# Starting the next stage's normalisation and weights in the tail of the stage ahead, in a four-stage f32 kernel

## The reference

```python
x = x + attention0(layernorm(x))   # linear attention with decay, 32 heads of 128, gated
x = x + ffn0(layernorm(x))         # SwiGLU, 1376 hidden, with LoRA of rank 16
x = x + attention1(layernorm(x))   # ALiBi softmax, causal, 32 heads of 16, q and k normalised
x = x + ffn1(layernorm(x))         # GELU, 2048 hidden

def _layernorm(x, axis=-1, eps=1e-05):
    m = jnp.mean(x, axis=axis, keepdims=True)
    v = jnp.var(x, axis=axis, keepdims=True)
    return (x - m) / jnp.sqrt(v + eps)
```

## Time and profile before

| | us |
|---|---|
| median of 3 runs | 2022.02 |
| lowest, highest | 2015.08, 2023.35 |
| profiled execution | 2025.39 |
| its span | 2023.7 |
| PE busy | 1916.9 |
| DVE busy | 856.4 |
| POOL busy | 610.3 |
| ACT busy | 437.1 |

### The profile page before, as it was taken

The page is one execution under the profiler, slowest core; times in us unless marked ns, Lnnn a source line. Parts: engine busy times, 40 slices in busy tenths (PEclk is TensorE's granted clock), DMA queues, the critical chain, the costliest instruction groups (busy, mean ns, idle before and its releaser), DMA issues. The chain is left out here.

```text
span 2023.7 us, 26337 instructions
## 1 busy us (share of the span) xinstructions
PE 1916.9 (95%) x10439; PEld 1504.0 (74%) x10439; DVE 856.4 (42%) x1586; ACT 437.1 (22%) x534; POOL 610.3 (30%) x692
## 2 busy tenths in 40 slices
PE   6999999999999999999999869998888999987999
PEld 5888888888888888888888758886653444456887
DVE  5242342432433333424324453313666888725611
ACT  3111111111111111111111121101313666643200
POOL 4322231321312313222300045534720212225532
PEclk9999999999999999999999979998985999998999
DMA  4010100110110100101100112201033233001111
GB/s 157 29 58 29 58 29 29 57 57 10 47 57 29 54 32 30 56 29 57 36 0 16 47 53 83 81 7 69 21 66 51 48 54 55 14 22 47 50 50 68
DMA packets 36521, 93.15 MB, mean 46 GB/s; under 512 B 7200, under 2 KB 11936, under 8 KB 31968
## 3 DMA queue, kind: packets, MB, share of 16 engines
q1 hardware_dynamic: 35172, 89.56, 15.1%
q10 hardware_dynamic: 1276, 2.62, 0.8%
HBM read 75.89 MB, written 2.10 MB: 39 GB/s over the span
## 5 line engine op out<-in xcount | busy, mean ns | idle before, releaser
L146 PE MATMUL a_ps<-a_xh_h,a_w_h 128*128 128x512 f32 x768 | 307.4, 400 | 4.3 <-POOL a_w_l L270 2.9
L148 PE MATMUL a_ps<-a_xh_h,a_w_l 128*128 128x512 f32 x768 | 301.3, 392 | 0.0
L147 PE MATMUL a_ps<-a_xh_l,a_w_h 128*128 128x512 f32 x768 | 300.7, 391 | 0.0
L60 POOL TENSOR_TENSOR tick<-neg_half 128x1 f32<-128x1 f32 x48 | 24.6, 513 | 615.7 <-PE a_ps L148 615.7
L390 DVE TENSOR_TENSOR x<-x,a_ps 128x1024 f32<-128x1024 f32 x64 | 78.2, 1221 | 259.9 <-PE a_ps L148 259.9
L1153 ACT ACTIVATE a_pr<-a_ps 128x1024 f32<-128x1024 f32 (+1 forms) x192 | 153.1, 812 | 88.3 <-PE a_ps L1366 71.4
L146 PEld LDWEIGHTS a_ps<-a_xh_h,a_w_h 128*128 128x128 f32 x768 | 145.0, 189 | 32.5 <-issue 3.3
L148 PEld LDWEIGHTS a_ps<-a_xh_h,a_w_l 128*128 128x128 f32 x768 | 144.6, 188 | 30.4
L147 PEld LDWEIGHTS a_ps<-a_xh_l,a_w_h 128*128 128x128 f32 x768 | 144.9, 189 | 27.9
L146 PE MATMUL a_ps<-a_w_h,a_xh_h 128*128 128x512 f32 x352 | 145.0, 412 | 8.7 <-POOL a_w_l L251 5.9
L1386 PE MATMUL a_ps<-a_K,a_Q 64*128 64x512 f32 (+2 forms) x384 | 136.8, 448 | 14.1 <-DVE a_mx L1261 11.5
(11 more groups left out here) (180 smaller groups left out, 3651.9 us busy)
## 6 DMA issues: line engine op xcount, KB each, us to landing
a_raw<-in_a_wqkgv SPq DMA_DIRECT2D x30, 1024.0 KB, 4.9
f_raw<-in_f_w SPq DMA_DIRECT2D x33, 320.0 KB, 2.9
a_raw<-in_a_wout SPq DMA_DIRECT2D x32, 256.0 KB
f_raw<-in_f_w SPq DMA_DIRECT2D x32, 256.0 KB, 2.6
a_cst<-in_a_cst SPq DMA_DIRECT2D x32, 129.0 KB, 2.0
...
```

The source lines that it names most:

```text
L60: nc.gpsimd.tensor_tensor(top["tick"][:, :], top["neg_half"][:, 0:1], top["neg_half"][:, 1:2], ALU.mult)
L146: nc.tensor.matmul(out, w_hi, x_hi, start=start, stop=False)
L147: nc.tensor.matmul(out, w_hi, x_lo, start=False, stop=False)
L148: return nc.tensor.matmul(out, w_lo, x_hi, start=False, stop=stop)
```

## The change

**Normalisation.** The helpers take a list of tiles. The first tiles of the next stage's normalisation (`F0_EARLY` and `F1_EARLY` four, `A1_EARLY` five) are done in the block ahead, each as soon as its part of `x` is final: DVE alternates `x_out` or `add_out`, statistics and subtractions, each `x_out` or `add_out` with a wait for its own end; the other engines get the matching steps. The rest (`..._LATE`) is done at the start of the next stage, behind PE's first products. `xh_h`, `xh_l` and the first weights (high, low and raw) become shared buffers in `top`; placeholders named `under_...` keep the stages' own buffers off them.

**First weights.** SP loads ffn0's LoRA matrix and first two weight blocks in attention0, attention1's q weights in ffn0, and the first two blocks of ffn1 in `attention1_out`; POOL splits them there, ahead of `rms` in attention0 and between the last `split_w2` in ffn0.

**Semaphores.** These steps have a second `Sems` object in attention0, ffn0 and `attention1_out`, each with its own clearing and meeting of all engines at the end.

**Output of ffn0.** The last two f are one loop over the output tiles, with the transpositions of tile i-4 behind tile i.

**Attention1.** `FIRST` is gone: m = 0 and 1 start at once, and tiles 5, 6 and 7 are transposed ahead of m = 2, 3 and 4. The q-side stacks of pairs 3 to 5 (30 transfers) are issued by SP, not by ACT. POOL clears their tiles, not DVE.

```diff
@@ attention0: SP, POOL, DVE
+            sp.wait_ge(s("proj_done"), 16 * NG)
+            sp.dma_start(top["f0_la"][:, :], a["f0_lora_a"]).then_inc(s2("la_in"), 16)
+            for w in (1, 3):
+                sp.dma_start(top[f"f0_raw{w}"][:, :], a[f"f0_w{w}"][0]).then_inc(s2(f"raw{w}_in"), 16)
             sp.wait_ge(s("attn_done"), H0)
...
+            f0_split_a(nc, pool, s2, top)
+            for w in (1, 3):
+                pool.wait_ge(s2(f"raw{w}_in"), 16)
+                f0_split_w(nc, pool, s2, top, w, 0)
             pool.wait_ge(s("ms_ready"), 1)
...
+            for t in F0_EARLY:
+                ln_gpsimd(nc, pool, s2, b, F0_EARLY, t)
...
-            for t in range(NT):
+            def x_out(t):
                 nc.vector.scalar_tensor_tensor(out=x[:, t, :], in0=acc[:, t, :], scalar=rms[:, t:t + 1],
                                                in1=x_again[:, t, :], op0=ALU.mult, op1=ALU.add).then_inc(s("x_out"), 1)
-            dve.wait_ge(s("x_out"), NT)
+                dve.wait_ge(s("x_out"), t + 1)
+            ln_vector(nc, dve, s2, b, F0_EARLY, x_out, lambda t: x_out(t + 4))
@@ ffn0: POOL, DVE, PE
             for f in range(2, NF0):
                 split_w2(f)
+                if 4 <= f < 4 + KT:
+                    split_next(f - 4)
+            for t in A1_EARLY:
+                ln_gpsimd(nc, pool, s2, b2nd, A1_EARLY, t)
...
+            ln_vector(nc, dve, s2, b2nd, A1_EARLY, add_out, lambda t: add_out(t + 3) if t >= 2 else None)
...
-            ln_tensor(nc, pe, s, b, range(4))
             lowered(0)
-            ln_tensor(nc, pe, s, b, range(4, 6))
             hidden(1, 0, 0)
-            ln_tensor(nc, pe, s, b, range(6, NT))
+            ln_tensor(nc, pe, s, b, F0_LATE, F0_LATE)
             lowered(1)
...
-            for f in range(NF0):
+            for f in range(NF0 - 2):
...
+            pe.wait_ge(s("w2_split"), NF0)
+            pe.wait_ge(s("g_split"), 2 * NF0)
+            for i in range(NT):
+                out(NF0 - 2, i)
+                out(NF0 - 1, i).then_inc(s("out_done"), 1)
+                if i >= 4:
+                    ln_tensor(nc, pe, s2, b2nd, A1_EARLY, (i - 4,))
+            ln_tensor(nc, pe, s2, b2nd, A1_EARLY, (4,))
@@ attention1_heads: SP, POOL, ACT, DVE, PE
             stack(sp, 3, 0)
+            stack(sp, 3, 1)
             max_row(1)
-            stack(sp, 4, 0)
-            stack(sp, 5, 0)
+            for p in (4, 5):
+                stack(sp, p, 0)
+                stack(sp, p, 1)
...
+            pool.wait_ge(qs("proj_done"), 3 * NT)
+            for i in range(3, SETS):
+                nc.gpsimd.memset(QT[i].bitcast(F32)[:, :], 0.0).then_inc(s("late_clear"), 1)
...
-            for p in range(3, SETS):
-                stack(act, p, 1)
...
-            pieces(1, 2, 8)
-            dve.wait_ge(qs("proj_done"), 3 * NT)
-            for i in range(3, SETS):
-                clear(i)
-            pieces(1, 8, NP)
+            pieces(1, 2, NP)
...
+            for m in range(AFTER):
+                if 2 <= m < 2 + len(A1_LATE):
+                    ln_tensor(nc, pe, qs, b, A1_LATE, (A1_LATE[m - 2],))
@@ attention1_out: DVE, PE
+            ln_vector(nc, dve, s2, b, F1_EARLY, add_out, lambda t: add_out(t + 4))
...
                 part(t, 3).then_inc(s("out_done"), 1)
+                if t >= 4:
+                    ln_tensor(nc, pe, s2, b, F1_EARLY, (t - 4,))
@@ ffn1: PE
-            ln_tensor(nc, pe, s, b, range(4))
-            pe.wait_ge(s("ln_lo"), 4)
             hidden(0, 0)
-            ln_tensor(nc, pe, s, b, range(4, NT))
-            pe.wait_ge(s("ln_lo"), NT)
+            ln_tensor(nc, pe, s, b, F1_LATE, F1_LATE)
+            pe.wait_ge(s("ln_lo"), len(F1_LATE))
             hidden(0, 1)
```

More of the change, by code:

```diff
@@ L49 @@
 NF1 = F1 // P
+ALL = range(NT)
+F0_EARLY, F0_LATE = range(4), range(4, NT)
+A1_EARLY, A1_LATE = range(5), range(5, NT)
+F1_EARLY, F1_LATE = range(4), range(4, NT)
+XH = 2 * KT * T
+EARLY = 3 * KT * D
 def split_hi(engine, hi, src):
@@ L106, in ln_gpsimd @@
-def ln_gpsimd(nc, pool, s, b, t):
-    one = slice(t, t + 1)
-    pool.wait_ge(s("ln_meanvar"), t + 1)
+    for i in range(min(ahead, len(tiles))):
+        stats(i)
+    for i, t in enumerate(tiles):
+        if i + ahead < len(tiles):
+            stats(i + ahead)
+        dve.wait_ge(s("ln_hi"), i + 1)
+        nc.vector.tensor_tensor(b["xh_l"][:, :, t * P:(t + 1) * P], b["bank"](t).rearrange("p (k q) -> p k q", k=KT),
+                                b["xh_h"][:, :, t * P:(t + 1) * P], ALU.subtract).then_inc(s("ln_lo"), 1)
+        if after is not None:
+            after(t)
@@ L138, in ln_tensor @@
+def ln_tensor(nc, pe, s, b, tiles, some):
+    for t in some:
+        pe.wait_ge(s("ln_normed"), tiles.index(t) + 1)
         for k in range(KT):
-            last = nc.tensor.transpose(b["ps"][:, t, k * P:(k + 1) * P], b["xn"][:, t % 2, k * P:(k + 1) * P],
+            last = nc.tensor.transpose(b["bank"](t)[:, k * P:(k + 1) * P], b["xn"][:, t % 2, k * P:(k + 1) * P],
                                        b["ident"][:, :])
@@ L686, in _ @@
             split_a2(0)
-            split(3, 0)
             for f in range(1, NF0):
@@ L1105, in select @@
                                         ).then_inc(s("selected"), 1)
-            for t in range(NT):
-                ln_gpsimd(nc, pool, qs, b, t)
-                if FIRST - 1 <= t < FIRST - 1 + KT:
-                    split(0, (t - FIRST + 1,))
+            for t in A1_LATE:
+                ln_gpsimd(nc, pool, qs, b, A1_LATE, t)
             split(1)
@@ L1537, in _ @@
                 sp.dma_start(raw[:, w], w_dram[:, w]).then_inc(s(f"raw_in{k}"), 16)
+            for i in range(2):
+                sp.dma_start(top["f1_raw"][:, i, :], w1_dram[i]).then_inc(s2(f"raw_in{i}"), 16)
         @block.gpsimd
```

365 lines of the change are left out of this document (200 added, 165 removed).

## The result

The changed kernel takes 2008.8 us (median of 9 runs, 1998.1 to 2011.2) where the kernel before takes 2022.3: ratio 0.992, 95% interval 0.9901 to 0.9939. Forecast were 2004.0 us and a range of 1995 to 2013. Its profiled execution took 2008.8 us, span 2007.0, so 16.6 less than the span before (2023.67 and 2007.03), where 18.0 were forecast.

What follows compares the result with a forecast made beforehand. PE, busy 95% of the span, bounds the kernel; only its idle time and half-clock work can move. Terms -0.8 - 5.6 + 0.8 - 6.4 - 6.5 + 0.5 = -18.0 us gave median 2004.0, range 1995 to 2013.

Steps and rivals of the forecast that it cites:

- Stage ends: Freeing semaphores at stage ends: 65 ranges for 29 at 0.16 us, three more meetings at 0.3, +6.7 us of PE idle.
- Attention0 to ffn0: From attention0's end to `lowered(1)`: DVE's chain takes 1.6 and 1.4 us a tile, `lowered(1)` starts earlier, -0.8 us.
- `lowered(1)` starts at 1197.95: In ffn0, after 5.2 us for tiles 4 to 7, `lowered(1)` starts at 1197.95 for 1198.75.
- Ffn0 to attention1: From ffn0's end to attention1's first clip: -7.3 us, with 1.7 of clock loss -5.6; bounds -8 and -2.5.
- I charge another 1.7: In ffn0, a clock loss of 1.7 us behind PE's new 2.2 us stall before step 9.
- Heads: In attention1, with the stacks on SP, PE's 6.36 us idle before the third score go: -6.4 us, bounds 0 and -9.5.
- I count nothing for them: In attention1, moving the three memsets to POOL gains nothing, since PE is then held by pair 1's row.
- Projection to ffn1: From the projection's last matmul to `hidden(0,1)` of ffn1: start at 1838.5 for 1844.98, -6.5 us; bounds -3.8 and -8.5.
- (a): Rival: in quad 0 the clock rises 13 to 15 us sooner, up to 7 us more gain, about 1997; chance 0.18.
- (b): Rival: boundaries give little, four-tile chains need 7.9 us, freed blocks run at half clock, ranges cost 0.25; 2012, chance 0.17.
- (c): Rival: in the heads the stacks don't pay, another thing holding the exponential or the maxima: +6.4, 2010.5 us; chance 0.12.
- (d): Rival: slower, the clock doesn't rise at 1560 but stays at half through quad 1: +25, 2029 us; chance 0.04.

Runs made afterwards that it cites:

- e11: The changed kernel, unaltered, timed again beside other runs on another chip: median 1999.4 us, ratio 0.9890 to the kernel before.
- e6: The changed kernel, but DVE clears the tiles of pairs 3 to 5, not POOL; SP still issues the stacks: 2007.4 us, ratio 0.992.
- e4: The kernel before with the heads' part alone: q-side stacks of pairs 3 to 5 issued by SP, their tiles cleared by POOL: 2014.7 us, ratio 0.9957.

## Why the prediction was right, and where it was not

**Time and sign.** 2004.0 were forecast, 2008.8 measured; -18.0 in the profiled execution, -16.6 measured. That the total is so near is in part luck. Each term counted over the stretch that it was made for, the six measured -1.0 (for -0.8), -6.8 (-5.6), +0.35 (+0.8), -8.7 (-6.4), -5.2 (-6.5) and +0.45 (+0.5): together -20.9, almost 3 us more than the forecast. Blocks at half clock that stand in no term of the sum took 4.5 us back, 1.6 in ffn0, 1.3 in quad 1 and 1.6 in ffn1; all else comes to -0.2. And 2008.8 is the median of nine runs that spread over 13 us; e11's median of the same kernel is 9 lower.

**Stage ends.** The gaps grew by 1.69, 1.5, 0.35 and 1.95 us, at the end 0.45: 5.9 for 6.7. The price of 0.16 was near: the one clear stretch, behind the projection, has 1.10 us for one range, 1.58 for five and 1.96 for seven, 0.12 to 0.19 a range. After the heads five more ranges cost 0.35 and not 0.8.

**Attention0 to ffn0.** -0.98 for -0.8: the chain of 1.6 and 1.4 us a tile is in the trace. The step that failed is "`lowered(1)` starts at 1197.95": there the account stopped. The 5.2 us of transpositions that I moved together are a stretch in which PE is mostly idle, and 1.6 us at half clock came behind it. I had charged such a loss to the stall at step 9, where it did not come, and none here, where every trace of this order has it. Its bounds did not help: -2.5 to +2 were for the four tiles' time and for `lowered(0)`'s clock, and nothing behind `lowered(1)` was counted.

**Ffn0 to attention1.** Counted from the product behind `lowered(1)`, -6.8 for -5.6. The stall was 2.19 for 2.2. "I charge another 1.7" was wrong: the matmuls behind it are 0.23 apart, though a stall of 2.3 us elsewhere did bring the clock down in six traces of ten. DVE's tail was 0.8 longer than worked out: its subtractions wait 0.3 to 0.9 us for ACT, and the last additions stand behind them in DVE's queue. Without the 1.7 the account said -7.3.

**Heads.** -8.7 for -6.4 up to the third score. "I count nothing for them" (the clearings) is the step that failed: SP's row of pair 1 did hold the second score, by 0.96 us, as the prediction had it, but it came itself 1 us sooner, and PE did the maxima that DVE had held up ahead of it; e6 puts the clearings at 1.8 us. POOL's clearings ran beside DVE's reductions and did not slow them. Timeline of DVE in the changed kernel under the clearings (1502.34 to 1505.07):

```profile
1502.63 0.68 DVE L1273 TENSOR_SCALAR a_v<-a_ps 128x512 f32<-128x512 f32 x1
1503.23 1.28 DVE L1324 TENSOR_REDUCE a_mx<-a_ps 128x1 f32<-128x512 f32 x2
1504.43 0.27 DVE L1337 CAST a_crow<-a_ps 16x128 fp32r<-16x128 f32 x1
```

The same instructions in e6, where POOL does nothing beside them:

```profile
1500.35 0.68 DVE L1270 TENSOR_SCALAR a_v<-a_ps 128x512 f32<-128x512 f32 x1
1500.95 1.28 DVE L1321 TENSOR_REDUCE a_mx<-a_ps 128x1 f32<-128x512 f32 x2
1502.15 0.27 DVE L1334 CAST a_crow<-a_ps 16x128 fp32r<-16x128 f32 x1
```

The prediction's "By it the memsets would hold DVE" read the page too widely. The Trainium skill ("SBUF — State Buffer", Who interferes with whom) lets one block the other where both need the shared port pair, and has a DVE instruction with at most one input in SBUF, outside its modes with two ports, need it not. The trace agrees: these instructions read PSUM and take 0.68, 1.28 and 0.27 us with and without memsets beside them.

**Projection to ffn1.** -5.2 for -6.5, counted from the first product of the projection, and 1.57 lost behind it. The chain of the late tiles took 5.2 us, as worked out (1821.08 to 1826.31), while the gap was 3.53 for 3.15; what is missing is `hidden(0,0)`, 4.8 us for 4.2, DVE's tail, 0.5 longer, and the 0.4 of the gap. The prediction's own terms add up to 1838.35, not the 1838.5 that it gives.

**Rivals.** (a) happened in some executions and not in the profiled one: in e4 and e11 the clock rose 9 us behind the first score, some 15 us sooner than in the profiled execution, and that was worth 4.2 us, where up to 7 were worked out for 13 to 15 us. That PE was busy without a break and still at half clock, in the earlier trace rows and in the changed kernel from 1530 to 1540, remains. (b) happened in part: 1.6 us each in ffn0 and ffn1 by half clock, while the four-tile chains took 5.2 us, as forecast, and not 7.9. (c) fell: the stacks paid. (d) did not happen: in no trace did the low clock last through quad 1.

**Signs.** PE's wait for `w_l` was 2.2 us. The stages began 3.0, 3.0 and 3.5 us behind DVE's last instruction, with products. From DVE's end to `lowered(1)`, the first clip and `hidden(0,1)` it was 15.1, 18.2 and 13.5 us for 15.2, 18.5 and 12.7. The clock in quad 0 rose 24.4 us behind the first score where it had been 30.8, so 6.4 sooner, as forecast. One sign failed: ACT's table load stood 1.3 us behind the first score, not at or before it.
